# Output projection of a chunked state-space block: fp32 product against three products of rounded halves

## What is computed

```
x   = layernorm(x)
gate, hbc, dt = split(x @ in_proj_w)
xs, B, C = split(silu(causal_conv(hbc, 4 taps)))
M   = exp(cum_i - cum_j), lower triangle of a chunk, times C.B
Y   = M @ (dt * xs)  +  exp(cum) * (C @ state)      # inside the chunk, and from the chunks before
y   = (Y + D * xs) * silu(gate)
out = (y * rsqrt(mean(y * y) + eps) * norm_w) @ out_proj_w     # 4096 -> 256
x   = x + out
```

## Time and profile before

| | |
|---|---|
| median of three runs | 1578.11 us |
| the profiled run, its own time | 1578.13 us |
| its span | 1576.2 us |
| TensorE busy over the span | 1397.1 us (89%) |
| VectorE busy | 1241.6 us (79%) |
| ScalarE busy | 1015.2 us (64%) |
| GpSimd busy | 627.9 us (40%) |
| `out_proj`, 512 records | 241.1 us |

### The profile page before, as it was taken

The page is one execution under the profiler, slowest core; times in us unless marked ns, Lnnn a source line. Parts: engine busy times, 40 slices in busy tenths (PEclk is TensorE's granted clock), DMA queues, the critical chain, the costliest instruction groups (busy, mean ns, idle before and its releaser), DMA issues. The chain is left out here.

```text
span 1576.2 us, 26558 instructions
## 1 busy us (share of the span) xinstructions
PE 1397.1 (89%) x8760; PEld 1098.1 (70%) x8760; DVE 1241.6 (79%) x2732; ACT 1015.2 (64%) x2077; POOL 627.9 (40%) x449
## 2 busy tenths in 40 slices
PE   1989968438999999999999999999999999988898
PEld 1988857326767767777767777677677767765787
DVE  4763362628999998998999899899999989996533
ACT  1013321518888788888788888888887888872332
POOL 0000001012565555556545655645655655563000
PEclk9999976769999999999999999999999999997999
DMA  3020012052654443654444545445554434444000
GB/s 107 1 120 1 0 54 13 1 163 67 124 109 112 104 108 98 111 119 105 110 101 106 112 112 115 104 98 104 119 116 103 116 97 97 103 110 181 0 27 27
DMA packets 110587, 140.78 MB, mean 89 GB/s; under 512 B 32800, under 2 KB 59008, under 8 KB 109952
## 3 DMA queue, kind: packets, MB, share of 16 engines
q1 hardware_dynamic: 108352, 137.14, 36.8%
q10 hardware_dynamic: 2112, 2.10, 0.4%
HBM read 127.01 MB, written 12.19 MB: 88 GB/s over the span
## 5 line engine op out<-in xcount | busy, mean ns | idle before, releaser
L884 ACT ACTIVATE M<-cum_row,row 128x128 f32<-128x128 f32 x1024 | 311.8, 388 | 0.0
L1008 DVE SCALAR_TENSOR_TENSOR xs<-psum,conv_row,xs 128x511 f32<-128x511 f32 (+2 forms) x384 | 283.1, 737 | 7.6 <-ACT xs L900 7.5
L969 POOL TENSOR_TENSOR hid<-hid,sg 128x512 f32<-128x512 f32 x128 | 277.5, 2168 | 0.1
L963 POOL TENSOR_TENSOR xend<-xdt,row 128x512 f32<-128x512 f32 x128 | 134.7, 1053 | 319.5 <-DVE xdt L1018 319.5
L1185 PE MATMUL psum<-hid,wo 128*128 128x512 f32 x512 | 241.1, 593 | 0.3 <-POOL hid L969 0.3
L958 POOL TENSOR_TENSOR squares<-squares,sq 128x512 f32<-128x512 f32 x128 | 163.8, 1280 | 136.1 <-ACT sq L860 135.4
L1026 DVE TENSOR_TENSOR M<-M,CB 128x1024 f32<-128x1024 f32 x128 | 180.8, 1413 | 0.0
L860 ACT ACTIVATE sq<-hid 128x512 f32<-128x512 f32 x128 | 80.2, 627 | 125.0 <-POOL hid L969 125.0
L1147 PE MATMUL psum<-xend,B_tok 128*128 128x128 f32 x1024 | 137.1, 277 | 13.3 <-POOL xend L963 13.3
L1185 PEld LDWEIGHTS psum<-hid,wo 128*128 128x128 f32 x512 | 95.7, 188 | 73.3 <-issue 62.7
L38 PE MATMUL psum<-xT_hi,gw_hi 128*128 128x512 f32 x256 | 115.4, 451 | 29.3 <-POOL gw_lo L952 28.3
(11 more groups left out here) (170 smaller groups left out, 3100.2 us busy)
## 6 DMA issues: line engine op xcount, KB each, us to landing
cum_row<-cum_scratch SPq DMA_DIRECT2D x256, 256.0 KB, 4.5
e_row<-e_scratch SPq DMA_DIRECT2D x256, 128.0 KB, 3.7
xw_raw<-L_attn_in_proj_w_dram SPq DMA_DIRECT2D x32, 128.0 KB, 3.2
gw_raw<-L_attn_in_proj_w_dram SPq DMA_DIRECT2D x16, 256.0 KB, 6.1
wo_raw<-L_attn_out_proj_w_dram SPq DMA_DIRECT2D x32, 128.0 KB, 3.1
table_scratch<-table SPq DMA_DIRECT2D x1, 2176.0 KB, 11.1
row<-table_scratch SPq DMA_DIRECT2D x32, 64.5 KB, 3.2
x_res<-_attn_hidden_states_dram ACTq DMA_DIRECT2D x4, 512.0 KB, 10.5
```

Source lines behind the costliest of these rows:

```text
L884: last = nc.scalar.activation(M[:, v % 4, h, c * CH:(c + 1) * CH], cum_row[:, v % 2, h, c * CH:(c + 1) * CH], ACT.Relu, bias=scalar_of(G, ...
L963: nc.gpsimd.tensor_tensor(xend[:, v % 2], xdt[:, v % 4], per_chunk_head(G, TO_END, v), ALU.mult).then_inc(xend_done, 1)
L969: nc.gpsimd.tensor_tensor(hid[:, v % 2, :], hid[:, v % 2, :], sg[:, v % 8, :], ALU.mult).then_inc(hid_done, 1)
L1008: nc.vector.scalar_tensor_tensor(xs[:, v % 8, shift:], psum[:, X_BANK + v % 2, 0:TT - shift], tap_of(G, v, tap), xs[:, v % 8, shift:], ALU ...
```

## The change

`out_proj` becomes three products of rounded halves, like the in-projection. For that, the gated tile and the scaled weights are split: ScalarE makes `hid_hi` and `wo_hi` with a Copy, GpSimd makes `hid_lo` and `wo_lo` with a subtraction. `hid_to_hi` is the first thing of a slot on ScalarE, ahead of `square`; `hid_to_lo` is the first of a slot on GpSimd, ahead of `add_squares`. The weights' splits stand at the end of slots 13, 14, 15 and of slot 0 of the next group. `out_proj` waits for `hid_lo` where it waited for the gated tile, `skip_path` waits for `hid_lo` where it waited for `out_proj`, `wo` has two buffers, and the rings of M and xdt have three. `split_matmul` is at L36.

```
-    wo = sb("wo", [P, GP, D], F32)
+    wo = sb("wo", [P, 2, D], F32)
+    wo_hi = sb("wo_hi", [P, GP, D], F32R)
+    wo_lo = sb("wo_lo", [P, GP, D], F32R)
-    xdt = sb("xdt", [P, 4, CPT, 2, HP], F32)
+    xdt = sb("xdt", [P, 3, CPT, 2, HP], F32)
-    M = sb("M", [P, 4, 2, TT], F32)
+    M = sb("M", [P, 3, 2, TT], F32)
+    hid_hi = sb("hid_hi", [P, 2, TT], F32R)
+    hid_lo = sb("hid_lo", [P, 2, TT], F32R)
...
+            def hid_to_hi(G, v):
+                act.wait_ge(hid_done, nth(G, v))
+                act.wait_ge(out_done, nth(G, v - 2))
+                nc.scalar.activation(hid_hi[:, v % 2, :], hid[:, v % 2, :], ACT.Copy).then_inc(hid_hi_done, 1)
+
+            def wo_to_hi(G, j):
+                act.wait_ge(wo_done, G * GP + j + 1)
+                act.wait_ge(out_done, nth(G, j - GP))
+                nc.scalar.activation(wo_hi[:, j, :], wo[:, j % 2, :], ACT.Copy).then_inc(wo_hi_done, 1)
...
-                act.wait_ge(diag_done, nth(G, v - 4))
+                act.wait_ge(diag_done, nth(G, v - 3))
...
             def slot(G, u, last):
                 if live(u, 0, last):
+                    hid_to_hi(G, u)
                     square(G, u)
...
+                    if u >= 13:
+                        wo_to_hi(G + 1, u - 13)
+                if G > 0 and u == 0:
+                    wo_to_hi(G, GP - 1)
...
+            def hid_to_lo(G, v):
+                pool.wait_ge(hid_hi_done, nth(G, v))
+                pool.wait_ge(out_done, nth(G, v - 2))
+                nc.gpsimd.tensor_tensor(hid_lo[:, v % 2, :], hid[:, v % 2, :], hid_hi[:, v % 2, :].bitcast(F32),
+                                        ALU.subtract).then_inc(hid_lo_done, 1)
+
+            def wo_to_lo(G, j):
+                pool.wait_ge(wo_hi_done, G * GP + j + 1)
+                nc.gpsimd.tensor_tensor(wo_lo[:, j, :], wo[:, j % 2, :], wo_hi[:, j, :].bitcast(F32),
+                                        ALU.subtract).then_inc(wo_lo_done, 1)
...
             def slot(G, u, last):
                 if live(u, 0, last):
+                    hid_to_lo(G, u)
                     add_squares(G, u)
...
-                dve.wait_ge(diag_done, nth(G, v - 4))
-                dve.wait_ge(xend_done, nth(G, v - 4))
+                dve.wait_ge(diag_done, nth(G, v - 3))
+                dve.wait_ge(xend_done, nth(G, v - 3))
...
-                dve.wait_ge(out_done, nth(G, v - 2))
+                dve.wait_ge(hid_lo_done, nth(G, v - 2))
...
-                dve.wait_ge(out_done, nth(G, j - GP))
+                if G * GP + j >= 2:
+                    dve.wait_ge(wo_lo_done, G * GP + j - 1)
...
-                pe.wait_ge(hid_done, nth(G, v))
-                pe.wait_ge(wo_done, G * GP + j + 1)
+                pe.wait_ge(hid_hi_done, nth(G, v))
+                pe.wait_ge(hid_lo_done, nth(G, v))
+                pe.wait_ge(wo_lo_done, G * GP + j + 1)
...
-                    last = nc.tensor.matmul(psum[:, OUT_BANK + m, :], wo[:, j, m * P:(m + 1) * P], hid[:, v % 2, :],
-                                            start=(j == 0), stop=(j == GP - 1))
+                    cols = slice(m * P, (m + 1) * P)
+                    last = split_matmul(nc, psum[:, OUT_BANK + m, :], wo_hi[:, j, cols], wo_lo[:, j, cols],
+                                        hid_hi[:, v % 2, :], hid_lo[:, v % 2, :], start=(j == 0), stop=(j == GP - 1))
```

More of the change, by code:

```diff
@@ L685, in macaron @@
     cum_in, e_in, xw_in, wo_in = [[sem(f"{n}{i}") for i in range(2)] for n in ("cum_in", "e_in", "xw_in", "wo_in")]
+    wo_hi_done, wo_lo_done, hid_hi_done, hid_lo_done = [sem(n) for n in ("wo_hi_done", "wo_lo_done", "hid_hi_done", "hid_lo_done")]
     row_in, conv_row_in = [[[sem(f"{n}{i}_{j}") for j in range(GP)] for i in range(2)] for n in ("row_in", "conv_row_in")]
@@ L690, in macaron @@
                 states_done, off_done, off_scaled, relu_done, exp_done, M_done, diag_done, v_done, hid_done, sq_done, squares_done,
-                out_done]
+                out_done, hid_hi_done, hid_lo_done]
     AHEAD = 16
@@ L880, in relus @@
                 act.wait_ge(row_in[group_of(G, v) % 2][j], loaded(G, v))
-                act.wait_ge(diag_done, nth(G, v - 4))
+                act.wait_ge(diag_done, nth(G, v - 3))
                 for h in range(2):
                     for c in range(CPT):
-                        last = nc.scalar.activation(M[:, v % 4, h, c * CH:(c + 1) * CH],
+                        last = nc.scalar.activation(M[:, (G * SLOTS + v) % 3, h, c * CH:(c + 1) * CH],
                                                     cum_row[:, v % 2, h, c * CH:(c + 1) * CH], ACT.Relu,
@@ L891, in decays @@
                 act.wait_ge(relu_done, nth(G, v))
-                nc.scalar.activation(M[:, v % 4], M[:, v % 4], ACT.Exp, scale=-1.0).then_inc(exp_done, 1)
+                nc.scalar.activation(M[:, (G * SLOTS + v) % 3], M[:, (G * SLOTS + v) % 3], ACT.Exp, scale=-1.0).then_inc(exp_done, 1)
             def evac_x(G, v):
@@ L907, in _ @@
                 split_g_hi(0, half)
+            for j in range(GP):
+                wo_to_hi(0, j)
             def slot(G, u, last):
                 if live(u, 0, last):
+                    hid_to_hi(G, u)
                     square(G, u)
@@ L962, in to_chunk_end @@
                 pool.wait_ge(states_done, nth(G, v - 2))
-                nc.gpsimd.tensor_tensor(xend[:, v % 2], xdt[:, v % 4], per_chunk_head(G, TO_END, v),
+                nc.gpsimd.tensor_tensor(xend[:, v % 2], xdt[:, (G * SLOTS + v) % 3], per_chunk_head(G, TO_END, v),
                                         ALU.mult).then_inc(xend_done, 1)
@@ L974, in _ @@
                 split_g_lo(0, half)
+            for j in range(GP):
+                wo_to_lo(0, j)
             def slot(G, u, last):
                 if live(u, 0, last):
+                    hid_to_lo(G, u)
                     add_squares(G, u)
@@ L987, in slot @@
                         split_x_lo(G + 1, u - 6)
+                    if u >= 13:
+                        wo_to_lo(G + 1, u - 13)
+                if G > 0 and u == 0:
+                    wo_to_lo(G, GP - 1)
             run(pool, slot)
@@ L1025, in masked @@
                 cb = CB[:, t * CPT:(t + 1) * CPT, :].rearrange("p c i -> p (c i)").unsqueeze(1).to_broadcast([P, 2, TT])
-                nc.vector.tensor_tensor(M[:, v % 4], M[:, v % 4], cb, ALU.mult).then_inc(M_done, 1)
+                nc.vector.tensor_tensor(M[:, (G * SLOTS + v) % 3], M[:, (G * SLOTS + v) % 3], cb, ALU.mult).then_inc(M_done, 1)
             def scan(G, v, c):
@@ L1072, in wo_scale @@
                 dve.wait_ge(conv_row_in[G % 2][j], loaded(G, 0))
-                dve.wait_ge(out_done, nth(G, j - GP))
-                nc.vector.tensor_scalar(wo[:, j, :], wo_raw[:, j % 2, :], conv_row[:, G % 2, j, 0:1], None,
+                if G * GP + j >= 2:
+                    dve.wait_ge(wo_lo_done, G * GP + j - 1)
+                nc.vector.tensor_scalar(wo[:, j % 2, :], wo_raw[:, j % 2, :], conv_row[:, G % 2, j, 0:1], None,
                                         ALU.mult).then_inc(wo_done, 1)
@@ L1172, in diag @@
                         last = nc.tensor.matmul(psum[h * HP:(h + 1) * HP, Y_BANK, c * CH:(c + 1) * CH],
-                                                xdt[:, v % 4, c, h, :], M[:, v % 4, h, c * CH:(c + 1) * CH],
+                                                xdt[:, (G * SLOTS + v) % 3, c, h, :], M[:, (G * SLOTS + v) % 3, h, c * CH:(c + 1) * CH],
                                                 start=False, stop=True, skip_group_check=True)
```

2 lines of the change are left out of this document (1 added, 1 removed).

## The result

The changed kernel takes 1669.16 us, median of 4 runs (1667.22 to 1671.10), against 1577.86 (1577.59 to 1581.45) for the kernel before in the same session: ratio 1.0573, interval 1.0553 to 1.0593 (here and below, the ratio is to the kernel before in the same session, and the interval is its 95% interval). Slower, as forecast, but by 91 us where 42 were forecast, and outside the range.

The account below looks back on a forecast made before the run. TensorE and VectorE, both nearly full, release each other in turn, neither the limit alone. Seven groups 32.6, last group's phase slots 2.3 and tail 7 add 42 us: 1620 us forecast (chance 0.64), range 1583 to 1650.

Parts of the forecast that it names:

- The sum: Whole kernel: 32.6 for seven groups, 2.3 for the last group's phase slots and 7 for its end, 42 us slower.
- rival (c): VectorE's halo pieces and mask products stall behind GpSimd's added work, 25 us on top of the forecast, 1645; chance 0.20.
- The new wait: Behind a phase slot out_proj waits 1.03 us for hid_lo, then states for xend: 1.83 lost, 1.15 net taken.
- the boundary: Third phase slot of a group, also splitting next group's weights: states 1.86 us later, 1.2 us net per group.
- gives back 0.33 each: In the two slots up to the next phase slot TensorE is back to back and returns 0.33 us each, 0.66.
- TensorE is the one that is late: Reason for taking 1.15 us lost per ordinary phase slot, between bounds of 0.5 (VectorE has slack) and 1.83.
- rival (a): Faster: out_proj's saving counts, VectorE's 42 waits for TensorE shorten by 0.33 us each, 17 us, 1561; chance 0.10.
- The mask product at 962.52: VectorE's mask product read as standing alone at 1.24 us, the duration used for its place before xend's end.
- States waiting for xend at all four: Sign that the forecast is right: behind all four phase slots of a group, states waits for xend.
- The tail: Last group's end, slots without projections: hid_lo lengthens the ring of gates, 3.5 to 9.5 us, 7 taken.
- Edits at nothing: Rings of three, wo_scale's wait and skip_path's wait cost nothing; a binding ring would cost 14 us in all.

Follow-up runs that it names:

- e1: Changed kernel with products of zeros on TensorE in three waits (ahead of out_proj of slots 9 and 13, off-diagonal product of slot 0): 1645.23 us.
- e12: Changed kernel, out_proj reading and awaiting high halves only, low half and square sum behind xend and gate on GpSimd, one sq buffer: 1640.91 us.
- e14: Changed kernel with halves of the slot behind each phase slot made early, that slot's square sum behind xend, and products of zeros on TensorE: 1624.17 us.
- e13: Changed kernel without work for halves (rounded tiles written directly, same product three times), plus two products of zeros at each of two places: 1575.08 us.
- e3: Kernel before with only the rings of three for M and xdt: 1577.84 us, ratio 1.000.
- e16: Changed kernel with all halves made in their places, but out_proj reads high halves alone and doesn't wait for the low ones: 1648.97 us.
- e15: Changed kernel, out_proj reading high halves only, unread low half and square sum behind xend and gate, two sq buffers: 1578.46 us.
- e5: Changed kernel without work for halves: gate and wo_scale write rounded tiles, out_proj adds the same product three times: 1587.63 us, ratio 1.0075.

## Why the prediction was wrong in size

**The sum.** The span grew by 1665.5 - 1576.2 = 89.3. Of it 22.0 went when TensorE's waits were filled (the span of e1 is 1643.5), which is the clock's part. The other 67.3 lie in e1 against before, counted from xdt to xdt on VectorE: first group 5.2, six groups of 7.84, last group 10.3, behind its last xdt 7.7, and 2.9 less ahead of the loop.

**The step that failed first: the argument that set rival (c) aside.** The sum has nothing for halo pieces, because "one block of 2.56 us can stall only one more piece, and a piece that waits out hid_lo gets in before the square sum". Halo pieces grew by 26.2 us (144.3 against 118.1), 3.9 per group; rival (c) had priced them at 25 on top. The argument is right at 974.91. But a later queue shifts every operation in it, not only the new one: at 963.18 the square sum meets a piece that it had missed before, and in the slot behind the wait of 0.81 us it is the gate, behind the late xend (VectorE, then GpSimd):

```profile
1015.60 1.30 DVE L1044 SCALAR_TENSOR_TENSOR xs<-halo,conv_row,xs 128x1 f32<-128x1 f32 x1
```

```profile
1015.62 1.26 POOL L1002 TENSOR_TENSOR hid<-hid,sg 128x512 f32<-128x512 f32 x1
```

The piece begins while xend still runs (until 1015.66 us), yet it doesn't get in ahead of the gate: it ends with it, and 0.21 us of work have become 1.30. So (c) was not a rival but a second term. Its amount came out right; that the places decide and not a rate, as the prediction noted beside it, is what 106.1 to 163.8 us of halo pieces show, at the same GpSimd work within 2% in e12 and e14.

**The step that failed second: TensorE's clock has no term.** Every duration of TensorE came from stretches at 1.00, and was used behind waits that were then forecast at 1 to 4 us. The falls took some 22 us of the span (24 between the medians). The trace of before had a row to ask: the longest wait of the earlier trace rows, 3.9 us, stands in the last group, and behind it the clock is 0.50 from 1400.99 to 1404.41 us.

```profile
1401.26 0.76 PE L1161 MATMUL psum<-CT,carry 128*128 128x128 f32 x2 [3.94 <-DVE hid L1059]
...
1403.10 1.69 PE L1147 MATMUL psum<-xend,B_tok 128*128 128x128 f32 x8
```

The off-diagonal product takes 1403.10 - 1401.26 = 1.84 us there, not 0.89. The steady part, with waits of up to 1.70 us, has no fall.

Forecast, halo pieces and clock add up to 42 + 26 + 22 = 90 of the 91 us. That it closes so well is in part luck, since the parts of the forecast came out unevenly:

**The new wait: right in place, its price too high, and the give-back not as told.** hid_hi and hid_lo came in the order worked out. Split by VectorE's slots (from the end of one to the end of the next), e1 against before: the boundary cost 3.69 in slot 9 less 2.26 and 0.29 in slots 10 and 11, 1.14 us (1.2 forecast); slot 5 cost 0.72, slot 13 2.05 and slot 1 0.00, where 1.15 each were forecast. Together that is 3.9 us per group against 4.65; the rest of the 7.84 is halo pieces, 1.04 in slot 0, 1.29 in slot 2 and 1.12 in slot 6 above all. But "gives back 0.33 each" didn't happen behind the ordinary phase slots: the slots behind 5 and 13 had no less idle time on VectorE. The choice behind it, "TensorE is the one that is late", is what e13 speaks against. The earlier trace rows had both nearly full; VectorE's waits were used for rival (a) only.

**A reading.** The mask product at 962.52 did not stand alone: GpSimd's gate lies beside it from 962.68 and took 2.22 us, against 1.26 at 1015.62 in the changed kernel. So the 1.24 us are those of a product that started first, not of one that had nothing beside it.

**"States waiting for xend at all four"** held at one in the changed kernel, behind slot 5. In e1, without falls, it held at three (0.64, 0.67 and 0.75 us). Where the clock fell, the slow off-diagonal product covered it.

**The tail.** The last group and what lies behind it were 18.0 us longer, against 9.3 forecast (2.3 + 7). Behind the last xdt it was 7.7, but counted behind the last skip path it was 5.3, so the 7 isn't confirmed by itself. Clock falls of the last group, which e1 does not fill, and halo pieces are in these 18.0; how much is open.

**Edits at nothing:** the rings did cost nothing (e3).

What stays open: how much of the 70 us between e16 and e15 is xend's place and how much the halo stalls. In the table 4.1 us per group are idle time and 3.1 halo pieces, but one feeds the other.

## What to carry to other kernels

Before crediting a faster product, ask who sets the pace of each slot: where another engine does, the saving becomes a wait, and here three waits per group were each followed by half the clock. When an operation is added to a queue, follow everything that stands behind it, and try the place behind those that others wait for; check the buffers that the later place holds: with low half (unread) and square sum ahead of xend the kernel took 70 us more than with both behind it, and the move without a second `sq` buffer gave 8. Read stalls between VectorE and GpSimd piece by piece; shifts of half a microsecond to 1.3 us moved them either way. Where a sum adds a wait, look in the trace for the row behind a wait as long.

## What the runs showed that I had not expected

The clock fell behind waits of 3.77, 1.88 and 2.89 us and not behind one of 0.81. But length alone doesn't decide: in e5 two waits of the same 1.84 us, at the same place of two groups, end in a product at full and at half clock. (The kernel before waits 1.53 us at this place and never falls there; the cheaper out_proj made the wait 0.31 longer.)

```profile
655.71 0.46 PE L1188 MATMUL psum<-CT,zero_state 128*128 128x128 f32 x2 [1.84 <-DVE hid L1086]
...
928.55 0.69 PE L1188 MATMUL psum<-CT,zero_state 128*128 128x128 f32 x2 [1.84 <-DVE hid L1086]
```

A fall behind out_proj's wait cost 1.67 us on the spot in slot 9: 2.54 - 1.38 in out_proj and 1.40 - 0.89 in the off-diagonal product.
